# Attention: stacked rows of q and k loaded with the repeated row as the inner dimension, and values multiplied in halves of 256 queries

## The reference

```python
q, k, v = (shape(layernorm(x) @ W.T) for W in (Wq, Wk, Wv))     # (8, 16, 512, 16)
scores = einsum('bhqd,bhkd->bhqk', q, k) * 16**-0.5 + bias[h, q, k]
ctx = einsum('bhqk,bhkd->bhqd', softmax(scores), v)
x = x + merge(ctx) @ Wo.T
x = x + ffn(layernorm(x))    # top 2 of 7 experts and a shared one, GELU
```

## Time and profile before

| | |
|---|---|
| median of 3 runs | 1061.87 us (1061.54 to 1061.93) |
| profiled execution | 1057.47 us |
| its span, first to last instruction | 1055.7 us |
| TensorE matmuls busy | 969.4 us (92%) |
| TensorE weight loads busy | 721.2 us (68%) |
| VectorE busy | 704.8 us (67%) |
| ScalarE busy | 514.2 us (49%) |
| TensorE clock granted, mean | 0.96 of full |

### The profile page before, as it was taken

One profiled execution on the slowest core, in us unless ns is written; L12 is line 12 of the kernel. 1 busy time (PEld: TensorE's weight loads), 2 busy tenths in 40 slices (PEclk: granted clock), 3 DMA queues, 4 the chain that ended last, 5 costly groups with the idle time before them and its releaser, 6 DMA issues. The chain is left out here.

```text
span 1055.7 us, 20280 instructions
## 1 busy us (share of the span) xinstructions
PE 969.4 (92%) x7264; PEld 721.2 (68%) x7264; DVE 704.8 (67%) x2048; ACT 514.2 (49%) x680; POOL 109.4 (10%) x245
## 2 busy tenths in 40 slices
PE   5799368999999998999999769999999999999998
PEld 3688145566655665566565449898988888888887
DVE  5565467777767777777786267676766666666764
ACT  3344015666656665666666635444434344444433
POOL 1120011111111111111111000000000000000000
PEclk9899559999999999999999969999999999999999
DMA  5997534323443333333334332010201020201000
GB/s 114 323 321 257 196 93 119 103 94 98 133 129 97 99 125 109 107 99 99 93 93 125 101 105 80 22 59 21 61 21 61 1 79 0 79 1 41 1 21 20
DMA packets 63923, 100.26 MB, mean 95 GB/s; under 512 B 9464, under 2 KB 37648, under 8 KB 63806
## 3 DMA queue, kind: packets, MB, share of 16 engines
q1 hardware_dynamic: 60594, 97.48, 29.3%
q0 software_dynamic: 3072, 1.11, 0.8%
q10 hardware_dynamic: 172, 0.56, 0.2%
HBM read 63.67 MB, written 34.93 MB: 93 GB/s over the span
## 5 line engine op out<-in xcount | busy, mean ns | idle before, releaser
L678 DVE CUSTOM_DVE_ANT_0 sums<-pS,near 128x512 bf16<-128x512 f32 x512 | 325.3, 687 | 125.4 <-PE pS L738 123.7
L709 ACT ACTIVATE prob<-pE 128x1024 f32<-128x1024 f32 x256 | 260.7, 1024 | 209.8 <-PE pE L763 209.3
L1185 PE MATMUL pD<-w2p,h_p 128*128 128x256 f32 x1536 | 203.0, 285 | 1.8 <-DVE x L1035 1.8
L738 PE MATMUL pS<-k_st,q_st 48*128 48x512 f32 x512 | 167.2, 497 | 40.6 <-DMA k_st<-k_parts 27.4
L1185 PEld LDWEIGHTS pD<-w2p,h_p 128*128 128x128 f32 x1536 | 191.4, 188 | 11.2 <-DVE x L1035 2.7
L763 PEld LDWEIGHTS pE<-bandT,place 64*128 64x128 f32 x2048 | 182.5, 190 | 16.1
L1167 PE MATMUL pU<-x2T,w1p 128*128 128x512 f32 x768 | 191.4, 399 | 0.0
L738 PEld LDWEIGHTS pS<-k_st,q_st 48*128 48x128 f32 x512 | 72.3, 193 | 171.5 <-DVE nmax L678 128.1
L1098 ACT ACTIVATE h_f<-pU,b1s 128x512 f32<-128x512 f32 x128 | 88.1, 688 | 191.5 <-PE pU L1167 185.7
L763 PE MATMUL pE<-bandT,place 64*128 64x244 f32 (+2 forms) x2048 | 180.1, 272 | 0.0
L1167 PEld LDWEIGHTS pU<-x2T,w1p 128*128 128x128 f32 x768 | 141.4, 190 | 29.4
(11 more groups left out here) (102 smaller groups left out, 575.1 us busy)
## 6 DMA issues: line engine op xcount, KB each, us to landing
x<-in_x SPq DMA_DIRECT2D x16, 512.0 KB, 4.5
q_parts<-qk SPq DMA_DIRECT2D x16, 512.0 KB, 5.0
k_parts<-qk SPq DMA_DIRECT2D x16, 512.0 KB, 4.7
q_st<-q_parts SPq DMA_DIRECT2D x64, 128.0 KB
k_st<-k_parts SPq DMA_DIRECT2D x64, 128.0 KB
ctx<-ctx_sb SPq DMA_DIRECT2D x32, 256.0 KB, 10.8
near<-bias_by_distance SPq DMA_DIRECT2D x16, 448.0 KB, 14.2
v_rows<-vs SPq DMA_DIRECT2D x8, 512.0 KB, 3.2
```

Of the source, the lines that this page charges most:

```text
L678: dve.tensor_tensor_reduce(sums[:, r % 4], pS[:, BANK[r]], near[:, hg % 2, j, lead:lead + S], -1.0, BIG, ALU.add, ALU.min, nmax[:, j, t:t ...
L709: act.activation(prob[:, par, 2 * step:2 * step + 2], pE[:, 2 * (step % 2):2 * (step % 2) + 2], ACT.Exp).then_inc(exp_done, 1)
L738: pe.matmul(pS[:, BANK[unit]], q_st[rows, r, pair, P * t:P * t + P], k_st[rows, r, pair], start=True, stop=True).then_inc(s_mm, 1)
L1185: ins = pe.matmul(pD[:, t2, u], h_p[:, e % 2, a, m, P * t:P * t + P], w2p[:, e, z, m], start=k == 0 and e < NE - 1, stop=k == 5)
```

## The change

Two edits. In `stacked` the repetition of rows becomes an inner dimension, behind the 16 rows: q's high rows come as row 0, row 0, row 1, row 1 and so on. For k the first 32 rows are now high and low in turn, taken from both parts by one DMA, and the last 16 are high, so that the same three products are summed in another order of rows. The number of DMAs, their sizes and their rows are as before.

In `values` each head's matmul of 512 queries becomes two of 256, `part` 0 and 1. One half is multiplied in each step, where before every odd step had a whole one. The semaphore that tells ScalarE and GpSimd of it rises at the end of the second half.

```diff
-    def stacked(t, b, hg, side, part, copies):
-
-        lead = ((b * 2 + part) * HG + hg) * (HPG * DH * S) + side * (2 * DH * S)
-        return bass.AP(t.tensor, lead, [[0, copies], [2 * S, DH], [1, 2 * S]])
+    PART = HG * HPG * DH * S
+
+    def stacked(t, b, hg, side, part, inner):
+
+        lead = (b * 2 + part) * PART + hg * (HPG * DH * S) + side * (2 * DH * S)
+        return bass.AP(t.tensor, lead, [[2 * S, DH], *inner, [1, 2 * S]])
...
-                         stacked(q_dram, b, hg, side, 0, 2)).then_inc(qk_ld[r], 16)
+                         stacked(q_dram, b, hg, side, 0, [[0, 2]])).then_inc(qk_ld[r], 16)
...
-                         stacked(q_dram, b, hg, side, 1, 1)).then_inc(qk_ld[r], 16)
-            sp.dma_start(raw(k_st[row:row + DH, r]).rearrange("p j s -> p (j s)"),
-                         stacked(k_dram, b, hg, side, 1, 1)).then_inc(qk_ld[r], 16)
-            sp.dma_start(raw(k_st[row + DH:row + KQ, r]).rearrange("p j s -> p (j s)"),
-                         stacked(k_dram, b, hg, side, 0, 2)).then_inc(qk_ld[r], 16)
+                         stacked(q_dram, b, hg, side, 1, [])).then_inc(qk_ld[r], 16)
+            sp.dma_start(raw(k_st[row:row + 2 * DH, r]).rearrange("p j s -> p (j s)"),
+                         stacked(k_dram, b, hg, side, 0, [[PART, 2]])).then_inc(qk_ld[r], 16)
+            sp.dma_start(raw(k_st[row + 2 * DH:row + KQ, r]).rearrange("p j s -> p (j s)"),
+                         stacked(k_dram, b, hg, side, 0, [])).then_inc(qk_ld[r], 16)
...
-                def values(n, par, t, first=False):
-
-                    if t == 0:
+                def values(n, par, t, part, first=False):
+
+                    queries = slice(QS * part, QS * part + QS)
+                    if t == 0 and part == 0:
...
-                        ins = pe.matmul(pC[32 * j:32 * j + 32], v_aug[:, par, t, j], prob[:, par, at],
-                                        start=t == 0, stop=t == TT - 1, skip_group_check=True)
-                    ins.then_inc(pv_done, 1)
+                        ins = pe.matmul(pC[32 * j:32 * j + 32, queries], v_aug[:, par, t, j], prob[:, par, at, queries],
+                                        start=t == 0 and part == 0, stop=t == TT - 1 and part == 1, skip_group_check=True)
+                    if part == 1:
+                        ins.then_inc(pv_done, 1)
...
-                        if step % 2 == 1 and not (first and u == 0):
-                            values(n - 1, (u + 1) % 2, step // 2, first and u == 1)
+                        if not (first and u == 0):
+                            values(n - 1, (u + 1) % 2, step // 2, step % 2, first and u == 1)
...
                 for t in range(TT):
-                    values(NI - 1, 1, t)
+                    for part in range(2):
+                        values(NI - 1, 1, t, part)
```

More of the change, by code:

```diff
@@ L553, in attend @@
         LEAD = 7
+        QS = S // 2
         PLACES = [*range(6), None, *range(6, 14), None, 14, 15]
```

## The result

The changed kernel takes 1036.7 us (median of 4, 1035.8 to 1038.2) where the one before takes 1061.7 beside it: ratio 0.9767, 95% interval 0.9750 to 0.9784. The forecast was 1034. By the medians that is 25.0 less; 27.8 less was forecast. The profiled execution has a span of 1035.5 us against 1055.7, only 20.2 less: the one of the kernel before took 1057.5 us, 4.2 under the median of 1061.7, the one of the kernel after 1037.3, 0.6 over its median. One execution of one experiment (split_copies) took 3678 us where the others took 1022 to 1023, and is left out. Most of what follows is about where forecast and measurement differ, and about the fact that one half of the change costs what a part of the other brings.

A forecast was written before the change was run, and what follows sets the result against it. TensorE's order was taken to set the pace, 13.4 us a unit. -21.8-22.6+13.3+3.3 = -27.8 takes the span from 1055.7 to 1027.9 us; with the median 6.2 over the span, 1034 us, range 1014 to 1054.

The forecast's parts named there:

- The loads, mechanism: Attention's q and k loads: sources beginning with 16 use all 16 DMA engines, two rows on each, not two engines.
- The loads, steady part: 29 attention units from 162.33 to 573.50: 13.4 us each in place of 14.18, no load wait left, -22.6 us.
- The start: Start of attention: SP freed, first exponential at 129 not 148.23, unit 1's at 140.5 not 162.33, -21.8 us.
- just in time: Unit 0's maxima leave at about 120 and need 5.6+2.5 us, before the first exponential at 129.
- The halves, steady part: Values in halves over 29 units: 0.46 us a unit from bank waits and the context copy, +13.3 us.
- The banks two back: Units 7 and 15 reuse the score bank of two back: 0.20 us wait, twice a unit, 0.40.
- The copy of the context: First values of a unit move to step 0 and wait for ScalarE's context copy: 0.06 us a unit.
- The last units: Last two units, without scores or bank wait to win: changeovers, weight loads and context copy cost +3.3 us.
- D: Values on TensorE: weight loads of halves stand in the open, 0.16 us a half, 1074 us; chance 0.06.
- B: Values in halves are cheaper: VectorE stays fed and changeovers shrink, 1007 to 1020 us; chance 0.17.
- C: Another wait takes the place in attention: maxima, first near loads or context copy, 1050 us; chance 0.14.
- E: The q and k loads stay on two engines, only the values edit acts, 1074 us; chance 0.06.

The follow-up runs named there:

- split_copies: Kernel before, its own row order, each load of a repeated part made as two DMAs of 16 rows: 1022.2 us, ratio 0.9666.
- k_two_engines: Kernel before, its own row order, q's repeated rows by two DMAs of 16 rows, k's sources still beginning with 2: 1031.2 us, ratio 0.9737.
- loads_only: Kernel before with only the changed q and k loads, values whole as before: 1021.1 us, ratio 0.9643 to the kernel before.
- more_bytes: loads_only plus two needless 512 KB loads of x ahead of the last batch's stores: 1023.1 us, ratio 0.9664 to the kernel before.
- banks_in_turn: Changed kernel with the three score banks taken strictly in turn in place of fixed places: 1024.5 us, ratio 0.9678 to the kernel before.
- halves_together: Changed kernel with both halves of values following each other in the odd step: 1023.3 us, ratio 0.9663 to the kernel before.
- scores_behind: loads_only with exponents ahead of scores in every odd step: 1014.9 us, ratio 0.9596 to the kernel before.
- near_late: loads_only with near tables 2 and 3 issued in attention, each behind one of the first two band loads: 1026.5 us, ratio 0.9701.

## Why the prediction was right, and where not

*The loads, mechanism.* Right, and shown: for the four loads of a unit, eight rows of 4 KB on each of 16 engines in place of 64 on each of two. split_copies has the gain without the new order of rows, and k_two_engines has a part of it with a part of the cause. That a leading broadcast confines a DMA, as the Trainium skill has it in "DMA: Bandwidth & Descriptors" (Rules for kernel authors), agrees with both.

*The loads, steady part.* -22.6 was forecast, -19.6 measured by loads_only. All the waits went, as said; the 13.4 us a unit was read from one turn (3.33), and the two behind it in the same trace take 3.43 and 3.35. Over 29 units it is 13.50, and that is the difference.

*The start.* This is the term that failed: -21.8 forecast, -15.3 measured. Two steps of it were wrong. The first was "attention begins when SP is through [...] Freed, 104.88 plus six issues of 0.45 is 107.6". SP was not freed: the issues take 2.14 and 2.62 us with the quick loads too, in sum 1.5 less than before. I had put them down to the two long queues, though all 16 DMA engines were as full there before, and I gave that row no weight:

```profile
107.60:112.00 4.40, 0.00 (x0) 0.00 (x0) 0.00 (x0) 0.00 (x0) 0.00 (x0) 0.50 0.99 365
```

VectorE starts at 113.5, where I had 109. What exactly blocks SP stays open: more_bytes shows that it is not simply the bytes ahead, since 1.0 MB more did not delay it. The second was what stands behind VectorE. The timelines of the kernel after:

```profile
113.53 0.69 DVE L681 CUSTOM_DVE_ANT_0 sums<-pS,near 128x512 bf16<-128x512 f32 x1 [10.06 <-PE pS L741]
...
133.00 0.69 DVE L681 CUSTOM_DVE_ANT_0 sums<-pS,near 128x512 bf16<-128x512 f32 x1
...
133.96 1.01 PE L758 MATMUL pE<-q_st,k_st 62*128 62x512 f32 x2
134.53 1.05 PE L766 MATMUL pE<-bandT,place 64*128 64x154 f32 x7
```

The line of 133.00 is the 14th side of unit 1; with it the last scores ahead of the first exponents get their bank. From VectorE's start to its end it is 20.2 us, and I had 20.1, though put together otherwise: I had 1.5 for unit 1's loads, which hold nobody now, and nothing for the turning of unit 0's maxima (0.7) and the bank gaps (three of 0.35). But from that side's end, 133.7, to the first exponential, 135.83, TensorE needs 2.1 us more for the exponents and bands at a granted clock of 0.50, and my sum has the exponential at the very end of the 14 sides. In the kernel before the same stretch takes 2.1 as well (146.1 to 148.23). 4.5 and 2.1, with the 0.1 between, make the 6.8 by which the first exponential missed 129, to rounding. Unit 0 itself was right (11.2 against 11.5), and so was "just in time": its maxima have landed at 133.7.

*The halves, steady part.* +13.3 forecast, +11.1 measured. A changeover more in place of the bank wait, to nothing: right; steps are 1.64 to 1.70 where I had 1.67. The banks two back: 0.40 a unit forecast; two steps of 1.91 for 1.67, 0.48, shown by banks_in_turn. The copy of the context: 0.06 a unit forecast, and not there in the changed kernel; it lies behind the bank wait, and shows as 0.10 once that is gone. I had added two delays of which one hides the other. The rest is again the pattern, 13.50 for 13.4, which the halves were set against.

*The last units.* +3.3 forecast; its terms (8 x 0.33 and 2 x 0.26) add up to 3.2. Measured +3.5 to the end of the program, of which 3.1 is in the last units themselves. That fits in size; no run takes these terms apart, and none shows the 0.1 for a weight load in the open by itself.

*The rivals.* D (weight loads in the open) falls with the step, 0.67 a half as forecast, and with halves_together: 1.00 us as for whole values. The strict reading of the rule in the Trainium skill, "TensorE: Matmul & The Clock Gate" (The mechanism), that weights load only beside other row groups, would have made it 1.16, an estimate with the 0.16 of the earlier trace rows. B (cheaper halves) falls with the gaps, which are still 0.13 behind and 0.10 ahead. C did not come: no wait for maxima is in the list after, up to unit 30. E fell with the landings.

*The total.* The terms miss by 7.6 us in the traces: 6.5 at the start, 0.9 in the steady part (3.0 for the loads, less 2.2 for the halves, to rounding), 0.2 at the end. The medians miss by only 2.7, because the kernel before was profiled in an execution 4.2 us under its median and the sum was set on the median; that 1036.7 lies so near 1034 is in part luck. The range, 1014 to 1054, would not have held the kernel with no gain at the start (1056) or none in the steady part (1057), but it would have with halves that cost nothing (1017).

*What the profile was to show.* Right: no wait for `k_st` behind 130 us, the context in 2.6 us, steps of 1.67 and two of 1.9, value records of 0.39. Wrong: the first exponential near 129 (135.8). Not as said: a DMA share over 0.5 behind the issues; 0.41 is what the one window has.

## What to carry to other kernels

Before a DMA with a broadcast is written, look at the size of the source's first dimension; and when unrelated transfers land at several times their best while the DMA share sits at a small fraction of 16, look for one that uses a few engines. Splitting a block of matmuls to smooth the work buys a changeover per piece, here 0.23 us against a removed wait of 0.26, so nothing was to be won; and it brought out a bank that is used again after two products, which whole values had hidden. Moving the waiting instruction past others that are ready (scores_behind) removes the same wait without a changeover, but only together with banks in turn does it pay in full (987.6 us). A line that says what an engine waited for is to be held against the time at which that thing landed, as near_late shows. And measure the two halves of a change apart: one of them was worth 1.3% with the wrong sign.

## What had not been expected of the hardware

Matmuls of 256 columns in twice the number, with twice the weight loads, took the same time as 512 columns (1.00 us a group, four side by side). And 1.0 MB more in front of the last stores delayed their landing by 3.7 us. That is more than the 2.8 that the 377 GB/s of the kernel after would give, and about what the run's own rates give (338 GB/s from 104 to 112 us and 303 from 112 to 120: 3.1 to 3.5). But SP's next issues became quicker: 2.35 us for the two near tables where they took 2.62. How SP's issue time follows the state of the queues is left open.
